# Attention output of both layers: eight-column denominators, placement by feature with DMAs, division of whole blocks

## The reference

```
# layer 0, k and v repeated over 4 heads each
scores = jnp.einsum('bhqd,bhkd->bhqk', q, k) / jnp.sqrt(jnp.float32(hd))
attn = jax.nn.softmax(scores, axis=-1)
attn = jnp.einsum('bhqk,bhkd->bhqd', attn, v)
attn_out = attn.transpose(0, 2, 1, 3).reshape(B, L, D) @ Wo
# layer 1, causal
attn = jnp.where(causal_mask[None, None], -jnp.inf, attn)
attn = jax.nn.softmax(attn, axis=-1)
```

## Time and profile before

| what | us |
|---|---|
| median of 3 runs | 1913.61 (1909.39 to 1915.45) |
| the profiled execution | 1912.95 |
| its span | 1911.1 |
| PE busy | 1649.7 (86%) |
| DVE busy | 1478.6 (77%) |
| ACT busy | 1350.1 (71%) |
| POOL busy | 888.5 (46%) |

### The profile page before, as it was taken

How to read it: one execution, slowest core, us unless ns; L and a number is a source line. 1 busy time by engine, 2 the same in 40 slices (tenths; PEclk the granted TensorE clock), 3 DMA queues, 4 the chain that set the end, 5 groups by cost and what they waited for, 6 DMA issues and landing times. The chain is left out here.

```text
span 1911.1 us, 45999 instructions
## 1 busy us (share of the span) xinstructions
PE 1649.7 (86%) x17410; PEld 874.4 (46%) x17422; DVE 1478.6 (77%) x1729; ACT 1350.1 (71%) x2673; POOL 888.5 (46%) x572
## 2 busy tenths in 40 slices
PE   6789999999788877777777669998999998999996
PEld 2235555555344444444444433433656556344442
DVE  3688899999299999999999975447888845556457
ACT  4417888888799999989999953443777773654443
POOL 1165666666099999999999981000000002000000
PEclk8858999999998888898888889996999999999998
DMA  2343444443489898888888942021222100000000
GB/s 117 123 160 139 157 154 161 159 153 141 141 312 315 314 315 298 311 279 292 302 322 296 305 150 88 12 73 42 47 37 45 29 4 18 1 1 0 0 6 17
DMA packets 82504, 278.86 MB, mean 146 GB/s; under 512 B 11159, under 2 KB 11954, under 8 KB 81311
## 3 DMA queue, kind: packets, MB, share of 16 engines
q1 hardware_dynamic: 68223, 225.67, 35.6%
q0 software_dynamic: 13824, 50.34, 6.8%
q10 hardware_dynamic: 288, 0.45, 0.1%
HBM read 214.72 MB, written 61.21 MB: 144 GB/s over the span
## 5 line engine op out<-in xcount | busy, mean ns | idle before, releaser
L1664 POOL TENSOR_TENSOR hc<-st,ct 128x1024 f32<-128x1024 f32 x256 | 598.2, 2374 | 8.2 <-DVE st L1623 7.7
L1623 DVE TENSOR_TENSOR_SCAN st<-da,banks 128x1024 f32<-128x1024 f32 x256 | 562.5, 2265 | 17.3 <-ACT da L1580 7.2
L528 ACT ACTIVATE attn_probs<-banks 128x512 f32<-128x512 f32 (+3 forms) x640 | 324.9, 534 | 93.3 <-PE banks L362 76.7
L362 PE MATMUL banks<-attn_qa,attn_ka 75*32 75x512 bf16 (+3 forms) x3584 | 347.9, 365 | 9.1 <-DMA attn_qa<-attn_mrow 2.8
L581 DVE TENSOR_REDUCE attn_mx<-banks 128x1 f32<-128x1024 f32 x256 | 309.8, 1223 | 32.7 <-PE banks L362 20.5
L1588 ACT ACTIVATE ut<-b_turned,mats 128x128 f32<-128x128 f32 x1024 | 311.7, 387 | 1.7
L362 PE MATMUL banks<-attn_ka,attn_qa 72*32 72x512 bf16 (+3 forms) x3584 | 291.3, 381 | 17.9 <-DVE attn_mx L578 11.0
L1580 ACT ACTIVATE da<-dt,mats 128x1024 f32<-128x1024 f32 x256 | 282.3, 1138 | 27.2 <-DVE st L1623 19.3
L1505 PE MATMUL banks<-hc,onecol 128*32 128x512 f32 x1024 | 159.5, 699 | 93.6 <-POOL onecol L1662 73.6
L759 POOL TENSOR_TENSOR made_ahead<-b_turned,x_turned 128x1024 f32<-128x1024 f32 x96 | 184.0, 1916 | 93.4 <-DVE attn_mparts L595 72.1
L578 DVE CUSTOM_DVE_ANT_0 banks<-banks,attn_maskwide 128x128 f32<-128x128 f32 (+7 forms) x256 | 191.1, 775 | 31.8 <-PE banks L362 28.4
(11 more groups left out here) (445 smaller groups left out, 1953.3 us busy)
## 6 DMA issues: line engine op xcount, KB each, us to landing
dt<-dt_rows SPq DMA_DIRECT2D x256, 512.0 KB, 5.6
ahead<-made_ahead POOLq DMA_DIRECT2D x96, 512.0 KB, 3.5
ua<-ahead SPq DMA_DIRECT2D x96, 512.0 KB, 5.9
attn_qa<-q_lin SPq DMA_DIRECT2D x144, 64.0 KB
attn_ka<-k_lin SPq DMA_DIRECT2D x72, 64.0 KB
moe_w<-in_moe_w SPq DMA_DIRECT2D x2, 2048.0 KB, 9.8
mats<-in_mats SPq DMA_DIRECT2D x1, 2988.5 KB, 13.1
xparts_kept<-xparts_lin SPq DMA_DIRECT2D x3, 512.0 KB, 3.7
```

The costliest lines, as they stand in the source:

```text
L362: last = nc.tensor.matmul(out[sl(t, 32), :], lhs[:, sl(t, 32)], rhs, start=start, stop=True, skip_group_check=True)
L528: nc.scalar.activation(probs[s % 4][:, jj, c0:BLK], scores_exp[jj][:, c0:BLK], ACT.Exp, scale=scale).then_inc(probs_ready, 1)
L1623: nc.vector.tensor_tensor_scan(st[n % 4][:, :], da[n % 4][:, :], pair[:, :, :].rearrange("p h t -> p (h t)"), 0.0, ALU.mult, ALU.add).then ...
L1664: nc.gpsimd.tensor_tensor(hc[n % 8][:, :], st[n % 4][:, :], ct[:, b * SEQ:(b + 1) * SEQ], ALU.mult)\
```

## The change

Nine things are done, in both attentions. (1) Columns 8 to 15 of the staged V are all one, so rows 8 to 15 of each group of 32 in `out_acc` hold the denominator eight times. (2) `turn_out` and `out_norm` are gone. (3) After each `out_copy` SP issues eight DMAs, four heads times numerators to `attn_t` and denominators to `den_t`, 8 partitions x 512 each (`out_rows`). (4) `den_t` is `ssm_in`, which had held `attn_tok`. (5) `out_copy` waits for the eight DMAs of the block before (`out_sent`), where it had waited for `turn_out`. (6) `turn_max` waits for ACT's copy of the other half's maxima, not for `out_norm`. (7) Once a 512-token block is complete, DVE inverts its 128 x 512 denominators in place and multiplies (`divide`); in attn1 it then adds the block to x. Three blocks are divided in the last unit's body, the fourth behind the last `out_copy`. (8) The final turning (line 503) and its four copies or additions are gone. (9) In SP's list `out_rows` of block 1 of the unit before stands behind the rows of half 1, `out_rows` of block 0 behind the first part of the loads, and the last `out_rows` ahead of `front.sync_third`.

```
-    nc.gpsimd.memset(vst[i][:, :, :, HD:HD + 1], 1.0).then_inc(vst_cleared, 1)
+    nc.gpsimd.memset(vst[i][:, :, :, HD:2 * HD], 1.0).then_inc(vst_cleared, 1)
...
+    def out_rows(i, qb):
+        g, b = units[i]
+        cols = slice(b * SEQ + qb * BLK, b * SEQ + (qb + 1) * BLK)
+        sp.wait_ge(osb_ready, 2 * i + qb + 1)
+        for j in range(4):
+            rows = sl(4 * g + j, HD)
+            sp.dma_start(attn_t[rows, cols], osb[32 * j:32 * j + HD, :]).then_inc(out_sent, 16)
+            sp.dma_start(den_t[rows, cols], osb[32 * j + HD:32 * j + 2 * HD, :]).then_inc(out_sent, 16)
...
     for i in range(UNITS):
         rows(i, 1)
+        if i > 0:
+            out_rows(i - 1, 1)
         if i + 2 < UNITS:
             load_part(i + 2, 0)
+        out_rows(i, 0)
...
+    out_rows(UNITS - 1, 1)
     front.sync_third(sp)
...
     def out_copy(i, qb):
         act.wait_ge(pv_done, NE * i + half_end[qb] + 1)
-        act.wait_ge(oturned, 2 * i + qb)
+        if 2 * i + qb > 0:
+            act.wait_ge(out_sent, 128 * (2 * i + qb))
         nc.scalar.copy(osb[:, :], out_acc[:, :]).then_inc(osb_ready, 1)
...
-    def turn_out(i, qb):
-        for t in range(4):
-            last = quad(turned[:, sl(t, TILE)], osb[:, sl(t, TILE)], k.m("ident"))
...
+    def divide(b, qb):
+        unit = max(i for i, u in enumerate(units) if u[1] == b)
+        blk = 2 * b + qb
+        dve.wait_ge(out_sent, 128 * (2 * unit + qb + 1))
+        num, den = attn_t[:, sl(blk)], den_t[:, sl(blk)]
+        taken[0] += 1
+        link(nc.vector.reciprocal(den, den), taken[0], inverted)
+        ins = nc.vector.tensor_tensor(num, num, den, ALU.mult)
+        if residual:
+            link(ins, taken[0], divided)
+            nc.vector.tensor_tensor(k.x[:, sl(blk)], k.x[:, sl(blk)], num, ALU.add)
...
-    if s == OUT_AT and i > 0:
-        out_norm(i - 1, 1)
-    if s == MID + 3:
-        out_norm(i, 0)
+    if i == UNITS - 1 and s in (12, 13):
+        divide(1 - last_b, s - 12)
+    if i == UNITS - 1 and s == MID + 7:
+        divide(last_b, 0)
```

More of the change, by code:

```diff
@@ L138, with attention @@
 K_ORDER = [0, 1, 2] * 3
-def attention(k, tag, q_lin, k_lin, k_heads, v, causal, attn_t, front, units, tok=None, residual=False,
+def attention(k, tag, q_lin, k_lin, k_heads, v, causal, attn_t, front, units, den_t, residual=False,
               probs=()):
@@ L247, in attention @@
         osb_ready = k.sem(f"{tag}_osb_ready")
[L248 to L249 removed]
+        out_sent = k.sem(f"{tag}_out_sent")
         own_dve = k.sem(f"{tag}_own_dve")
[L251 to L253 removed]
+        inverted = k.sem(f"{tag}_inverted")
+        divided = k.sem(f"{tag}_divided")
         vst = [k.sb(f"{tag}_vst{i}", [128, QT, nk, 32], F32, ctx) for i in range(2)]
@@ L381, in turn_max @@
                     pe.wait_ge(mparts_ready[half], i + 1)
-                    if i > 0:
-                        pe.wait_ge(normed, 2 * i - 1 + (half if not causal else 0))
-                    if causal and half == 1:
+                    if half == 1:
                         pe.wait_ge(mrow_ready[0], i + 1)
+                    elif i > 0:
+                        pe.wait_ge(mrow_ready[1], i)
                     for t in range(4):
@@ L495, in _ @@
                     pv_quad(UNITS - 1, NE - 2, vst[1], part)
[L496 to L505, removed]
             @block.scalar
@@ L560, in _ @@
                 out_copy(UNITS - 1, 1)
-                for n in range(NBLK if not residual else 0):
-                    act.wait_ge(final_turned, n + 1)
-                    nc.scalar.copy(attn_t[:, sl(n)], k.bank[n % 2][:, :]).then_inc(final_copied, 1)
             @block.vector
@@ L597, in combine @@
                     dve.wait_ge(mparts_ready[half], i + 1)
-                def out_norm(i, qb):
-                    dve.wait_ge(oturned, 2 * i + qb + 1)
-                    dve.wait_ge(normed, 2 * i + qb)
-                    tv = turned[:, :].rearrange("p (t j c) -> p t j c", t=4, j=4)
-                    link(nc.vector.reciprocal(rden[:, :, :], tv[:, :, :, 8]), 2 * i + qb + 1, own_norm)
-                    g, b = units[i]
-                    t0 = b * QT + 4 * qb
-                    dst = attn_tok[:, t0:t0 + 4, sl(g, 32)].rearrange("p t (j c) -> p t j c", j=4)
-                    nc.vector.tensor_tensor(dst, tv[:, :, :, 0:8],
-                                            rden[:, :, :].unsqueeze(3).to_broadcast([128, 4, 4, 8]), ALU.mult)\
-                        .then_inc(normed, 1)
+                def divide(b, qb):
[9 more added lines that the diff above has]
+                        nc.vector.tensor_tensor(k.x[:, sl(blk)], k.x[:, sl(blk)], num, ALU.add)
+                taken = [0]
+                last_b = units[UNITS - 1][1]
                 def body(i):
@@ L634, in _ @@
                     body(i)
-                out_norm(UNITS - 1, 1)
-                for n in range(NBLK if residual else 0):
-                    dve.wait_ge(final_turned, n + 1)
-                    nc.vector.tensor_tensor(k.x[:, sl(n)], k.x[:, sl(n)], k.bank[n % 2][:, :], ALU.add)\
-                        .then_inc(final_copied, 1)
+                divide(last_b, 1)
 class HybridFront:
```

16 lines of the change are left out of this document (removed).

## The result

| | before | after |
|---|---|---|
| median, us | 1914.43 (1909.39 to 1915.45, 4 runs) | 1983.63 (1979.78 to 1985.77, 4 runs) |
| span of the profiled execution | 1911.1 | 1983.9 |
| end of the last out_copy of attn0 | 509.96 | 541.54 |
| first DMA of the scan | 516.58 | 562.48 |
| first row DMA of attn1 | 1304.07 | 1348.30 |

The changed kernel is slower by the factor 1.0394 on record (95% interval 1.0368 to 1.0421). The medians of the table are 69.2 us apart, a factor of 1.036, and the spans of the two profiled executions 72.8 us. The forecast was 1914 and its range ended at 1940. The rows of the table cut the 72.8 us into pieces: +31.6 in the body of attn0, +14.3 at its end, -1.7 in the stages between (the first row DMA of attn1 is 44.2 later), +21.5 in the body of attn1, and +7.1 from its end to the end of the kernel.

A forecast was written before the change was run, and what follows sets the result against it. PE was taken to set the pace of both attentions. -26.1 + 9.5 + 12.5 + 1.2 + 4.0 = +1.1 us on the profiled 1912.95, 0.7 under the runs' median, gave 1914.0 us; range 1903 to 1940.

The forecast's parts named there:

- The small matmuls: PE's turn_out matmuls in both attentions, 15 each on PE's path at 0.87 us: removing them gives -26.1 us.
- Rival D: DVE, at 91% in attn0, catches up less, half the 26 us becomes waits on maxima: +14, 1927 us; chance 0.06.
- The hold-up of out_copy: Block 0's out_copy waits for eight new DMAs, 0.46 us per unit in attn0, 0.9 in attn1: +9.5 us, bounds 0 to 33.
- Rival B: SBUF-to-SBUF issues cost 0.578 us each, holding out_copy some 2.4 us in 14 units: +28, 1941 us; chance 0.27.
- The clock at the scan's start: Lower granted clock at the scan's start after idle PE: +1.5 us, of +4.0 for the clock at both ends.
- The end of attn0: From last out_copy, eight issues plus 16.0 us of reloads, 18.9 us against 6.34: +12.5 us.
- The end of attn1: After the last out_copy, issues, landing, reciprocal, multiplication and addition take 9.4 us against 8.19: +1.2 us.
- Both nothing; if the loads came late: In a unit, block 0's eight DMAs and block 1's out_copy cost nothing; loads over three slots late would make PE wait.

The follow-up runs named there:

- the probe: The kernel before with 26 extra DMAs at the end of SP's list in attn1, read for issue times only: 0.66 us SBUF to SBUF, 0.295 with DRAM.
- the copies on ACT: The kernel before with five useless copies on ACT ahead of out_copy of block 0 in 14 units: 1987.44 us, ratio 1.0422.
- the two experiments on the reloads: Kernel before, scan reloads held until attn0's last out_copy: 1916.27 us; changed kernel, reloads ahead of the last unit's block 0 output DMAs: 1971.20 us.

## Why the prediction was wrong

**The small matmuls: right.** -26.1 us was the size. Once nothing is in their place the unit is shorter by 1.7 us in attn0 (44.1 against 45.8) and by 1.7 in attn1 (29.8 against 31.5), twice 0.87. Rival D, that DVE would not follow, has nothing for it: PE's waits on maxima in 190 to 541 us are 3.3, as the 3.2 of the earlier trace rows.

**The hold-up of out_copy: the step that failed.** The mechanism, its place, the time at which the copy is due (263.20, measured 263.14) and the landing (2.2, measured 2.01) were right. The price of an issue was not: "I take 0.36, for out_rows reads and writes the same plain rows of 2 KB as the loads", where the probe shows that 8 x 512 costs 0.66 between SBUF and SBUF and 0.295 with DRAM on one side. The wait became 3.0 us and not 0.46 or 0.9, in 14 units 44.7 us of PE's time and not 9.5. Rival B had the kind of price right, at 0.578, and 33 us for it, with a chance of 0.27; its hold-up of 2.4 us was still short, since the issues follow each other at 0.67 and one in the unit above took 1.27.

**The clock behind each hold-up: missing from the sum.** The prediction had the row that shows it, 2.53 us instead of 1.23 after 5.41 idle, and used it at the two ends alone. It belongs wherever a term makes PE wait. With pauses of 3 us it cost 34.6 us in the profiled execution, 2.5 us a pause on average; the copies on ACT, with none of the DMAs, cost 35 over their own time, and filling the pauses brought 28 back. This is also why rival B, priced rightly at first sight, gave 1941: with 44.7 for the waits and 34.6 for the clock its sum would have been 28 - 33 + 44.7 + 34.6 = +74, against the 72.8 of the spans. The 34.6 were read off as what was left over in the bodies, so the agreement says only that the ends were near.

**The clock at the scan's start: shown, and gone again.** +1.5 was forecast. The first four matmuls took 3.78 us where they had taken 1.99, but the stages from there to attn1 are 1.7 us shorter in all, so nothing of the +1.5 is left in the time.

**The end of attn0: near.** +12.5 was forecast, 0.578 an issue made it 14.6, and 14.3 were measured; the traces of the two experiments on the reloads give 9.0 and 9.9 for their order alone. The reloads took 15.6 us against the 16.0 that were read from the earlier trace rows.

**The end of attn1: near, a little short.** +1.2 and +2.5 for the clock were forecast, 3.7 together; the chain to the first matmul is 3.3 longer and the eight matmuls 1.4 slower, 4.7. The reciprocal took 3.35 us where the rows gave 3.2. From the repeat count of 8 in the Trainium skill (VectorE: DVE Perf Modes, the first hardware budget of its walkthrough) an estimate of 4.3 us had been worked out; the trace has 3.35, and the measurement decides for the rows. What makes 4.7 into the 7.1 at the end of the kernel was not followed up.

**"Both nothing; if the loads came late".** The eight DMAs of block 0 cost next to nothing in the changed kernel, where the units were long anyway (PE waited 0.7 us for loads of q in attn1). As soon as the hold-up was gone, the two sets of eight together cost 12.9 us of waiting there. The zero rested on the wrong price too: at 0.67 two sets of eight fill 10.7 of 31.5 us.

## What to carry over

Price a DMA's issue by the memories at its two ends before its shape (on SP's queue here 0.62 to 0.66 us against 0.3), multiply by the number in a row, and look at what is queued behind the last of them. A wait that stops PE costs its own length and, at some 3 us, up to about as much again in the clock behind it; where the wait can't go, filling it helps. Many small DMAs can replace work on the bound engine, but only with a buffer to spare, and in the gaps of the issuing queue rather than around the loads that PE waits for.

## What the runs showed of the hardware

- SP's issue of an SBUF-to-SBUF DMA of 8 partitions took 0.625 us (median of 128) to 0.66 us (of four), and 0.588 at 16 and 32 partitions, against 0.295 with DRAM as source or target. On ACT's queue the same 8-partition DMA took 0.70 us, on POOL's 0.50.
- Pauses of 3.2 us, 14 times, took 80 us: the granted clock stood at 0.50 for the 6 us from 274 to 280 behind one. The same pauses filled with matmuls of no use left it at 1.00 in attn0.
- A reciprocal of 128 x 512 in fp32 on DVE took 3.35 us, a multiplication of this size 0.69.
- Three rows of maxima and twelve loads of 8 partitions, issued one behind the other within 6.2 us, landed late: PE, which waited for them, went on 7.5 us after the issue of the last. Issued alone and waited for, a DMA of 8 x 512 landed 2.0 us after the start of its issue between two places of SBUF, and 1.7 us after it with DRAM as its source.
- A transfer can also be late by what is queued ahead of it: with the reloads (ct, bt and xparts) issued directly before them, DVE waited for the eight output DMAs until 6.4 us behind the start of the issue of the last, and not 2.0.
